# Images 0 and 1 in a new order on all engines of a binarized Winograd convolution

## The chip, the cores and the metric

The kernel runs on one core of a Trainium2 chip. The metric is the time of one execution on the device in microseconds. Three executions of the kernel before gave a median of 950.4 us (949.73 to 950.79).

## The reference

The input is 16 images of 256 channels of 56 x 56 in fp32. What is computed, cut to its core:

```
v    = group_norm(x)                         # 32 groups, per image
xn   = batch_norm(v) * gamma + beta          # statistics over all 16 images
t    = sign(xn)                              # 1 or -1, never 0
csum = sum over channels of clip(xn, -1, 1) * t
y    = conv3x3(t, w) + b                     # 256 to 256 channels, padding 1
bmap = (box3x3(csum) + beta_b) / (box3x3(256) + beta_b)
out  = x + y * bmap
```

Both normalizations fold into one factor and one offset for each channel and image (tile AB), which are known only after all of x has been read once.

## The kernel before, in words

**Before the images.** Until about 151 us the kernel reads x once for the statistics (VectorE), and prepares the weights as fp16 pairs for a one-dimensional Winograd scheme (tile U, GpSimd and ScalarE). A chain of small VectorE operations ends at L721 with AB, the semaphore coef_ready. Then the 16 images are worked off, each in four groups g = 0 to 3. On the input side a group is one half h = g // 2 of the rows and one channel half c = g % 2. On the output side it is one half of the rows and one half of the output channels.

**Input side of a group.** ScalarE makes u = sign(AB * x) (`sign`, L385). `planes` (L395, L397) makes T = relu(2u) and T8 = 4T - 3. For image 0 VectorE makes T and T8 itself (L736, L741). VectorE's `transform` then makes differences (T with L739, tile D with L744 and L746) and from them the six planes of tile V (L750 for planes 0 and 1, L752 for positions 2 and 4, L753 for positions 3 and 5). T, T8 and D are single tiles. `v_ready` counts finished groups.

**Products.** TensorE runs 72 matmuls for a group in three sets of 24: `first`, `second`, `third`, each for two of the six planes, both channel halves, three horizontal shifts and two digits of the weights, accumulating in PSUM tile acc, of which there are two halves (b = g % 2). The first set needs just the V positions that L752 writes. A first set may begin when VectorE has emptied the bank two groups back (`y03_done`). Between the sets ScalarE copies acc to sn (`snapshot`, L427): second waits for the snapshot of the first set (snap1), third for the snapshot of the second (snap2). The order on TensorE is first(g), third(g-1), second(g).

**Output side.** `mid` (L790, L795, L797) combines the snapshots into two of the four output rows, `ends` (L806 twice) reads acc after the third set and gives the other two rows and y03_done, `finish` (L818) adds the bias and multiplies by the map bmap. GpSimd's queue then adds x by an accumulating DMA (L325) and stores (L320), two transfers of 784 KB for each group. SyncE does the last group's store.

**Channel sums.** ScalarE makes abs(xn) (`absolute`, L406) and a complement (L412), VectorE `pair_sum` (L760) joins the channel halves in ssum, `fold` (L767) reduces ssum to 49 columns of quarter for each half of the rows. TensorE's `quarter_sums` (L526) multiplies quarter by a folding matrix, one fp32 matmul for each half. ScalarE's `channel_sums` (L419) brings the result to cs49, SyncE stores it and reads it back by rows into crow (`crow_load`), and VectorE's `beta_map` (L773 to L782) makes the map, which SyncE stores and broadcasts to bmap.

**Order.** Each engine's order is written out by hand. Image 0 and parts of image 1 are straight code, then a loop runs over pairs of images. Each engine's queue is in order, so a waiting instruction holds all behind it. SyncE's queue holds the loads of x for image n + 2, crow_load, map_store and map_load. Image 0's order on TensorE before:

```
first(0, 0, 0, by_channels=True)
first(0, 0, 1)
second(0, 0, 0)
third(0, 0, 0)
second(0, 0, 1)
quarter_sums(0, 0)
quarter_sums(0, 1)
pe.wait_ge(v_ready, 4)
first(0, 0, 2)
```

With by_channels the first 12 matmuls use only channel half 0 and wait for v_ready 1, the next 12 for v_ready 2.

Of the kernel before, what the change touches and what calls it, by code (L numbers as in the profile page):

```python
# [42 lines left out]
def conv_preact(nc, x, w_t, gamma, beta, conv_b, beta_b, consts, sum_rows, map_rows, out):  # L43
# [6 lines left out]
    with ExitStack() as ctx:  # L50
# [3 lines left out]
        def sem(name):  # L54
# [18 lines left out]
        cs49 = sb("cs49", [NB, 2, SQ])  # L73
# [17 lines left out]
        ab = sb("ab", [P, 2, 2, CT])  # L91

        spare = ssum[:, :]
# [28 lines left out]
        ab_ready, u_ready, t_ready, t4_ready, t8_ready, cq_done, aq_done, v_ready = (  # L122
            sem(s) for s in ("ab_ready", "u_ready", "t_ready", "t4_ready", "t8_ready", "cq_done", "aq_done",
                             "v_ready"))
        quarter_ready = sem("quarter_ready")
# [47 lines left out]

        block = ctx.enter_context(nc.Block())
# [3 lines left out]
        def _(sp):  # L178
# [24 lines left out]
            def crow_load(m):  # L203

                sp.wait_ge(cs8_ready, m + 1)
                sp.dma_start(sum_rows[m, W:W + H * W].rearrange("(h k f) -> k h f", h=2, f=SQ), cs49[:, :, :])\
                  .then_inc(cs_stored, 16)
                sp.wait_ge(cs_stored, 16 * m + 16)
                at_least(sp, vsum_ready, m)
                sp.dma_start(crow[:, :, 1:W + 1], row_windows[m].rearrange("r (k w) -> r k w", w=W))\  # L210
                  .then_inc(crow_in, 16)

            def load(n, src, g):

                if g == 3:
                    sp.wait_ge(u_ready, 4 * n + 8)
                if g < 3 or isinstance(n, int) and n == 0:
                    sp.wait_ge(abs_done, 4 * n + g + 5)
                load_rows(src, g)

            def first_load(g):

                sp.wait_ge(u_ready, g + 1)
                sp.wait_ge(abs_done, g + 1)
                load_rows(x_rows[1], g)
# [30 lines left out]
            for g in range(G4):  # L256
                first_load(g)
            sp.wait_ge(zeros_in, 16)
# [4 lines left out]
            for g in range(G4):  # L263
                load(0, x_rows[2], g)
# [67 lines left out]
        def _(act):  # L332
# [56 lines left out]
            def planes(m, g):  # L389
# [4 lines left out]
                act.wait_ge(u_ready, s + 1)  # L394
                nc.scalar.activation(T[:, 30:60], u[:, g % 2, h:h + HR + 2], ACT.Relu, scale=2.0).then_inc(t_ready, 1)  # L395
                act.wait_ge(t_ready, s + 1)
                nc.scalar.activation(T8[:, :], T[:, 30:30 + HR], ACT.Copy, scale=4.0, bias=-3.0).then_inc(t8_ready, 1)  # L397

            def absolute(m, a, g):
# [3 lines left out]
                if g < 3:  # L403
                    act.wait_ge(u_ready, 4 * m + g + 1)
# [10 lines left out]
            def channel_sums(m):  # L415

                act.wait_ge(cs_done, 2 * m + 2)
                at_least(act, cs_stored, 16 * m)
                nc.scalar.activation(cs49[:, :, :].rearrange("p h f -> p (h f)"), csum[0:NB, 0:2 * SQ],  # L419
                                     ACT.Copy, bias=float(P)).then_inc(cs8_ready, 1)  # L420

            def snapshot(n, g, half):
# [3 lines left out]
                at_least(act, mid_done, s - 1)  # L426
                nc.scalar.activation(sn[:, b, half], acc[:, b, :, 0:N], ACT.Copy, scale=inv_s[:, b:b + 1])\  # L427
# [6 lines left out]
            sign(0, 0, 0)  # L434
# [32 lines left out]
            def image(n, a):  # L467
                for g in range(G4):
                    snapshot(n - 1, 3, 1) if g == 0 else snapshot(n, g - 1, 1)
                    planes(n, 3) if g == 0 else planes(n + 1, g - 1)  # L470
                    if g == 0:
                        channel_sums(n)
                        coefficients(n + 1, 1 - a)
                    snapshot(n, g, 0)
                    sign(n + 1, 1 - a, g)
                    for k in ((0,), (1,), (2, 3), ())[g]:
# [4 lines left out]
            with act.Fori(0, (NI - 2) // 2) as i:  # L481
                image(2 * i + 1, 1)
                image(2 * i + 2, 0)
            for g in range(G4):
                snapshot(NI - 2, 3, 1) if g == 0 else snapshot(NI - 1, g - 1, 1)
                if g == 0:
                    planes(NI - 1, 3)
                    channel_sums(NI - 1)
                snapshot(NI - 1, g, 0)
# [4 lines left out]
        def _(pe):  # L494
# [34 lines left out]
            def products(n, a, g, planes, done, by_channels=False):  # L529

                h, co = g // 2, g % 2
                for part in range(CT if by_channels else 1):
                    if by_channels:
                        pe.wait_ge(v_ready, part + 1)
                    for bank, k in enumerate(planes):
# [10 lines left out]
                last.then_inc(done, 1)  # L546

            def first(n, a, g, by_channels=False):

                at_least(pe, y03_done, 4 * n + g - 1)  # L550
                products(n, a, g, FIRST, first_done, by_channels)
# [11 lines left out]
            def image(n, a):  # L563
                for g in range(G4):
# [3 lines left out]
                    if g == 0:  # L568
                        quarter_sums(n, 0)
                        quarter_sums(n, 1)  # L570
# [29 lines left out]
        def _(dve):  # L600
# [123 lines left out]
            def transform(m, a, g):  # L724

                c, h, s = g % 2, g // 2, 4 * m + g
                pair = lambda at: T[:, at:at + 62].rearrange("p (j r) w -> p j r w", j=2)[:, :, 0:28:4]
                rows = lambda t, at: t.rearrange("p (q i) w -> p i q w", i=4)[:, at:at + 2]
                both = lambda at: D[:, :, at:HR:4]
                vk = lambda first, step: V[:, a, c, first:first + step + 1:step, h].rearrange(  # L730
                    "p k (q w) -> p k q w", w=W)
                at_least(dve, v_ready, s)
                at_least(dve, cq_done, s)
                if isinstance(m, int) and m == 0:
                    dve.wait_ge(u_ready, s + 1)
# [4 lines left out]
                if isinstance(m, int) and m == 0:  # L740
# [3 lines left out]
                nc.vector.tensor_tensor(rows(D[:, 1], 1), pair(3), pair(1), ALU.subtract).then_inc(aq_done, 1)  # L744
                dve.wait_ge(t8_ready, s + 1)
                nc.vector.tensor_tensor(D[:, 0], T[:, 32:32 + HR], T8[:, :], ALU.subtract).then_inc(cq_done, 1)  # L746
                if not (isinstance(m, int) and m <= 1):
                    dve.wait_ge(third_done, 4 * m - 6 + 2 * h)
                dve.wait_ge(cq_done, s + 1)
                nc.vector.tensor_tensor(vk(0, 1), rows(D[:, 0], 2), rows(D[:, 0], 0), ALU.subtract)  # L750
                dve.wait_ge(aq_done, s + 1)
# [176 lines left out]
```

## Time and profile before

| | |
|---|---|
| median of three executions | 950.4 us |
| the profiled execution's own time | 950.02 us |
| its span, first to last instruction | 948.0 us |
| PE busy with matmuls | 787.4 us, 83% |
| DVE busy | 790.3 us, 83% |
| ACT busy | 587.7 us, 62% |
| mean granted TensorE clock | 0.929 |

The profile is of one execution. PE is TensorE, PEld its weight loads, DVE VectorE, ACT ScalarE, POOL GpSimd and SP SyncE. In a timeline, consecutive instructions of one group are merged to a row with a count, and the bracket tells the idle time of the engine before it and what ended it. Matmul times overlap: a row of n matmuls lasts n steps and one latency, so a step is read from the starts of two rows. The granted clock is 1.00 at 2.4 GHz and 0.50 at 1.2 GHz. The shares of the whole span say little here, since the statistics stage ends near 151 us and the products only begin then.

### The profile page before, as it was taken

The page shows a single profiled execution, that of the slowest core. Times are in us where ns is not written, and L with a number is a line of the kernel's source. Part 1 is how long each engine was busy: PE and PEld are TensorE (multiplying, and loading weights), DVE is VectorE, ACT ScalarE, POOL GpSimd, SP SyncE. Part 2 cuts the span into 40 slices and gives each one's busy share as a digit, 9 for nine tenths or more (in the row PEclk, how much of TensorE's full clock was granted, in tenths as well). Part 3 has the DMA queues.
Part 4 walks back from the last instruction along what each step waited for, and adds up shares of the span by engine and source line. Part 5 has one row for each costly group of instructions (what it writes and reads, how often), then busy time and mean ns, then how long its engine had stood idle before and what let it go on. Part 6 is the DMA issues. An engine that isn't in the chain of part 4 may idle for free. (4 is left out here: it accounts for less than half of the span.)

```text
span 948.0 us, 12800 instructions
## 1 busy us (share of the span) xinstructions
PE 787.4 (83%) x4718; PEld 464.2 (49%) x4718; DVE 790.3 (83%) x1240; ACT 587.7 (62%) x472; POOL 141.2 (15%) x160
## 2 busy tenths in 40 slices
PE   2100003999999999999999999999999999999996
PEld 2100002555555555555555555555555555555553
DVE  4999997979879797979797979797979797979764
ACT  2043105796777777777777868686868686868410
POOL 0089300001111111111111111111111110101021
PEclk9655556999999999999999999999999999999998
DMA  9999972258978797969696969696969696968587
GB/s 361 428 402 378 418 291 71 74 207 239 281 201 283 173 309 167 314 165 303 169 309 166 305 169 302 175 282 188 285 193 287 185 289 190 280 167 208 134 237 239
DMA packets 43362, 232.76 MB, mean 246 GB/s; under 512 B 10448, under 2 KB 10576, under 8 KB 39248
## 3 DMA queue, kind: packets, MB, share of 16 engines
q0 software_dynamic: 18144, 101.16, 41.2%
q1 hardware_dynamic: 24432, 131.25, 38.4%
q10 hardware_dynamic: 768, 0.12, 0.1%
q8 instruction: 9, 0.15, 0.1%
q14 instruction: 9, 0.07, 0.0%
HBM read 180.73 MB, written 51.79 MB: 245 GB/s over the span
## 5 line engine op out<-in xcount | busy, mean ns | idle before, releaser
L540 PE MATMUL acc<-V,U 128*128 128x385 f16 (+1 forms) x4608 | 771.0, 330 | 18.4 <-DVE V L753 12.6
L540 PEld LDWEIGHTS acc<-V,U 128*128 128x128 f16 x4608 | 449.5, 98 | 333.9 <-issue 13.3
L427 ACT ACTIVATE sn<-acc,inv_s 128x784 f32<-128x784 f32 x128 | 116.8, 913 | 203.4 <-PE acc L540 200.2
L325 POOL DMA_DIRECT2D y<-x x63 | 53.9, 856 | 720.0 <-DVE y L818 706.5
L818 DVE SCALAR_TENSOR_TENSOR y<-y,vec,bmap 128x1568 f32<-128x1568 f32 (+1 forms) x65 | 117.5, 1810 | 0.4
L406 ACT ACTIVATE r<-xb,ab 128x1568 f32<-128x1568 f32 x64 | 106.5, 1690 | 6.7 <-DVE ssum L760 3.1
L385 ACT ACTIVATE u<-xb,ab 128x1624 f16<-128x1624 f32 x64 | 110.5, 1730 | 0.1
L395 ACT ACTIVATE T<-u 128x1680 f16<-128x1680 f16 x60 | 95.6, 1594 | 5.1 <-DVE D L746 5.0
L397 ACT ACTIVATE T<-T 128x1568 f16<-128x1568 f16 x60 | 90.6, 1511 | 1.9
L512 PE MATMUL csum<-mv,cst 128*128 128x32 f32 x2 | 0.6, 396 | 94.9 <-DVE mv L622 94.9
L746 DVE TENSOR_TENSOR D<-T 128x1568 f16<-128x1568 f16 x64 | 62.3, 974 | 18.1 <-ACT T L397 18.0
L790 DVE SCALAR_TENSOR_TENSOR ds<-sn 128x784 f32<-128x784 f32 x64 | 62.0, 969 | 6.6 <-ACT sn L427 6.6
L630 DVE BATCH_NORM_STATS2 st<-y 128x6 f32<-128x448 f32 x112 | 60.2, 601 | 6.2 <-DMA y<-x 6.1
L760 DVE SCALAR_TENSOR_TENSOR ssum<-r 128x1568 f32<-128x1568 f32 x32 | 57.3, 1792 | 8.2 <-issue 5.2
L630 DVE BATCH_NORM_STATS2 st<-xb 128x6 f32<-128x448 f32 x98 | 52.6, 600 | 6.8 <-DMA xb<-x 6.8
L767 DVE TRANSPOSE_TENSOR_REDUCE quarter<-ssum 128x49 f32<-128x1568 f32 x32 | 57.7, 1805 | 0.1
L320 POOL DMA_DIRECT2D out<-y x63 | 52.1, 826 | 29.3 <-DMA y<-x 28.8
L739 DVE TENSOR_SCALAR T<-T 128x784 f16<-128x784 f16 x64 | 22.5, 351 | 35.3 <-ACT T L395 35.2
L412 ACT ACTIVATE r<-r 128x1568 f32<-128x1568 f32 x32 | 48.3, 1511 | 1.0
L806 DVE SCALAR_TENSOR_TENSOR y<-acc,inv_s,ds 128x392 f32<-128x392 f32 x64 | 39.7, 621 | 10.0 <-PE acc L540 9.9
L512 PEld LDWEIGHTS csum<-mv,cst 128*128 128x128 f32 x2 | 0.5, 313 | 94.9 <-issue 94.9
L795 DVE SCALAR_TENSOR_TENSOR y<-sn,ds 128x392 f32<-128x392 f32 x64 | 36.4, 568 | 10.0 <-DMA out<-y 3.4
(92 smaller groups left out, 392.8 us busy)
## 6 DMA issues: line engine op xcount, KB each, us to landing
xb<-x SPq DMA_DIRECT2D x64, 812.0 KB, 6.4
y<-x POOLq DMA_DIRECT2D x63, 784.0 KB, 9.2
out<-y POOLq DMA_DIRECT2D x63, 784.0 KB, 9.3
y<-x SPq DMA_DIRECT2D x16, 1568.0 KB, 8.1
bmap<-map_rows SPq DMA_DIRECT2D x32, 784.0 KB, 5.9
xb<-x SPq DMA_DIRECT2D x14, 1568.0 KB, 8.4
V<-w_t SPq DMA_DIRECT2D x2, 1152.0 KB, 14.5
out<-y SPq DMA_DIRECT2D x2, 392.0 KB, 2.4
```

Source lines behind the costliest of these rows:

```text
L385: nc.scalar.activation(u[:, g % 2, 1:1 + XR], by_row(xb[:, c, g // 2]), ACT.Sign, scale=ab[:, a, 0, c:c + 1], bias=ab[:, a, 1, c:c + 1])\
L395: nc.scalar.activation(T[:, 30:60], u[:, g % 2, h:h + HR + 2], ACT.Relu, scale=2.0).then_inc(t_ready, 1)
L397: nc.scalar.activation(T8[:, :], T[:, 30:30 + HR], ACT.Copy, scale=4.0, bias=-3.0).then_inc(t8_ready, 1)
L406: nc.scalar.activation(r[:, c, 0:HPX], own_rows(g), ACT.Abs, scale=ab[:, a, 0, c:c + 1], bias=ab[:, a, 1, c:c + 1]).then_inc(abs_done, 1)
L427: nc.scalar.activation(sn[:, b, half], acc[:, b, :, 0:N], ACT.Copy, scale=inv_s[:, b:b + 1])\
L540: last = nc.tensor.matmul(by_row(acc[:, g % 2, bank, 0:N])[:, :, lo:hi], U[:, ci, digits, k, dx, co * P:(co + 1) * P], by_row(V[:, a, ci, ...
L630: ins = nc.vector.bn_stats(st[:, a, c, j], stat_buffer(a, c)[:, j * PIECE:(j + 1) * PIECE])
L746: nc.vector.tensor_tensor(D[:, 0], T[:, 32:32 + HR], T8[:, :], ALU.subtract).then_inc(cq_done, 1)
L760: nc.vector.scalar_tensor_tensor(out=ssum[:, :], in0=r[:, 0, 0:HPX], scalar=1.0, in1=r[:, 1, 0:HPX], op0=ALU.min, op1=ALU.subtract).then_i ...
L767: nc.vector.tensor_reduce(quarter[:, h, :], ssum[:, :].rearrange("p (b i) -> p b i", i=SQ), AX.X, ALU.add, apply_transpose=True).then_inc( ...
L790: nc.vector.scalar_tensor_tensor(out=ds[:, :, :], in0=sn[:, b, 0], scalar=2.0, in1=sn[:, b, 1], op0=ALU.mult, op1=ALU.subtract).then_inc(d ...
L818: nc.vector.scalar_tensor_tensor(out=y[:, g, lo:hi], in0=y[:, g, lo:hi], scalar=vec[:, 2, b:b + 1], in1=bmap[:, h, lo:hi], op0=ALU.add, op ...
```

## The change

Five things are changed for images 0 and 1, two for all images.

1. VectorE makes the signs of image 0's group 0 itself (`sign_first`, one fp32 comparison giving 1 or 0, with a one-column negation before it). ScalarE begins with group 1. u_ready is counted without group 0.
2. VectorE makes the differences of group 0 into D00 (a view of sn), writes its first planes (the L752 operation), then those of group 1 (v_first), and only then the other planes of both.
3. TensorE's first set of group 1 is split: plane 1 before second(0, 0, 0), plane 3 behind it. quarter_sums(0) moves behind first(0, 0, 2).
4. VectorE's and ScalarE's orders of images 0 and 1 are rewritten. VectorE makes T8 also for groups 1 and 2 of image 1. Image 1 and image 14 are taken out of the loops of those two engines; TensorE's loop stays.
5. SyncE issues the loads of image 2's groups 0 and 1 ahead of crow_load(0).
6. In all images the two folding matmuls become one with 98 columns of quarter, whose result lies on 98 partitions in cs98. In ScalarE's loop channel_sums stands behind snapshot(n, 0, 0) and no longer ahead of it.
7. In image 15, VectorE's finish of groups (14, 3), (15, 0) and (15, 1) come one step later each.

```
 TensorE
-            def quarter_sums(m, h):
-                pe.wait_ge(quarter_ready, 2 * m + h + 1)
-                if h == 0:
-                    at_least(pe, cs8_ready, m)
-                nc.tensor.matmul(csum[0:NB, h * SQ:(h + 1) * SQ], quarter[:, h, :], cst[:, C_FOLD:C_FOLD + SQ],
-                                 start=True, stop=True).then_inc(cs_done, 1)
+            def quarter_sums(m):
+                pe.wait_ge(quarter_ready, 2 * m + 2)
+                at_least(pe, cs8_ready, m)
+                nc.tensor.matmul(csum[0:2 * NB, 0:SQ], quarter[:, :, :].rearrange("p h b -> p (h b)"),
+                                 cst[:, C_FOLD:C_FOLD + SQ], start=True, stop=True).then_inc(cs_done, 1)
...
             first(0, 0, 0, by_channels=True)
-            first(0, 0, 1)
+            first(0, 0, 1, banks=(0,))
+            pe.wait_ge(v_ready, 2)
             second(0, 0, 0)
+            first(0, 0, 1, banks=(1,))
             third(0, 0, 0)
             second(0, 0, 1)
-            quarter_sums(0, 0)
-            quarter_sums(0, 1)
             pe.wait_ge(v_ready, 4)
             first(0, 0, 2)
+            quarter_sums(0)
 VectorE
+            def sign_first():
+                dve.wait_ge(x_in[0], 16)
+                chain(nc.vector.tensor_scalar(neg_b[:, :], AB[:, 0, 1, 0:1], -1.0, None, ALU.mult))
+                nc.vector.tensor_scalar(u[:, 0, 1:1 + XR], by_row(xb[:, 0, 0]), AB[:, 0, 0, 0:1], neg_b[:, 0:1],
+                                        ALU.mult, ALU.is_gt).then_inc(u0_ready, 1)
...
-            transform(0, 0, 0)
-            transform(0, 0, 1)
-            transform(0, 0, 2)
+            sign_first()
+            differences(0, 0, D00)
+            first_planes(0, 0, 0, D00).then_inc(v_first, 1)
+            differences(0, 1, D)
+            first_planes(0, 0, 1, D).then_inc(v_first, 1)
+            other_planes(0, 0, 0, D00)
+            other_planes(0, 0, 1, D)
             pair_sum(0, 0)
             fold(0, 0)
+            transform(0, 0, 2)
+            mid(0, 0)
             transform(0, 0, 3)
+            ends(0, 0)
             pair_sum(0, 1)
-            mid(0, 0)
-            ends(0, 0)
             fold(0, 1)
             mid(0, 1)
             transform(1, 1, 0)
-            beta_map(0)
             ends(0, 1)
             pair_sum(1, 0)
+            beta_map(0)
             transform(1, 1, 1)
             mid(0, 2)
             fold(1, 0)
-            transform(1, 1, 2)
             ends(0, 2)
+            finish(0, 0)
             pair_sum(1, 1)
             fold(1, 1)
-            finish(0, 0)
+            transform(1, 1, 2)
+            finish(0, 1)
+            mid(0, 3)
+            ends(0, 3)
+            transform(1, 1, 3)
+            beta_map(1)
...
+            finish(last - 1, 2)
+            mid(last, 0)
+            ends(last, 0)
+            finish(last - 1, 3)
+            mid(last, 1)
+            ends(last, 1)
+            finish(last, 0)
+            mid(last, 2)
+            finish(last, 1)
+            ends(last, 2)
+            finish(last, 2)
 ScalarE
             coefficients(0, 0)
-            sign(0, 0, 0)
             sign(0, 0, 1)
...
+            complement(0, 1)
+            snapshot(0, 0, 1)
             snapshot(0, 1, 0)
-            snapshot(0, 0, 1)
-            complement(0, 1)
             coefficients(1, 1)
             sign(1, 1, 0)
+            sign(1, 1, 1)
             planes(1, 0)
-            sign(1, 1, 1)
             snapshot(0, 1, 1)
-            channel_sums(0)
-            planes(1, 1)
-            snapshot(0, 2, 0)
             absolute(1, 1, 0)
             absolute(1, 1, 1)
+            snapshot(0, 2, 0)
+            channel_sums(0)
             complement(1, 0)
+            planes(1, 1)
             sign(1, 1, 2)
             snapshot(0, 2, 1)
-            planes(1, 2)
+            absolute(1, 1, 2)
             snapshot(0, 3, 0)
-            sign(1, 1, 3)
-            absolute(1, 1, 2)
             absolute(1, 1, 3)
             complement(1, 1)
+            planes(1, 2)
+            sign(1, 1, 3)
 SyncE
             for g in range(G4):
                 first_load(g)
+            load(0, x_rows[2], 0)
+            load(0, x_rows[2], 1)
             sp.wait_ge(zeros_in, 16)
             crow_load(0)
             map_store(0)
             map_load(0, 0)
             map_load(0, 1)
-            for g in range(G4):
-                load(0, x_rows[2], g)
+            load(0, x_rows[2], 2)
+            load(0, x_rows[2], 3)
```

## Rows read from the trace of the kernel before

**Rows 1.** waits of PE between 210 and 940 us (total us, times, longest us).

```profile
PE acc L540 <- DVE y L806: 1.6, 1, 1.6
```

**Rows 2.** timeline of PE, 150 to 235 us (start us, us, engine, line, operation, tiles, count, idle before).

```profile
158.32 3.51 PE L540 MATMUL acc<-V,U 128*128 128x392 f16 x12 [11.78 <-DVE V L753]
162.65 10.14 PE L540 MATMUL acc<-V,U 128*128 128x392 f16 x60 [0.83 <-DVE V L753]
173.80 8.15 PE L540 MATMUL acc<-V,U 128*128 128x392 f16 x48 [1.01 <-ACT sn L427]
...
190.79 12.13 PE L540 MATMUL acc<-V,U 128*128 128x392 f16 x72 [0.46 <-ACT sn L427]
...
208.75 4.16 PE L540 MATMUL acc<-V,U 128*128 128x392 f16 x24 [1.46 <-DVE y L806]
...
213.41 8.15 PE L540 MATMUL acc<-V,U 128*128 128x392 f16 x48
223.20 11.97 PE L540 MATMUL acc<-V,U 128*128 128x392 f16 x71 [1.64 <-DVE y L806]
```

**Rows 3.** timeline of PE inside the loop, 255 to 365 us.

```profile
311.42 0.37 PE L526 MATMUL csum<-cst,quarter 128*49 128x32 f32 x4
311.72 48.01 PE L540 MATMUL acc<-V,U 128*128 128x392 f16 x288
359.66 0.37 PE L526 MATMUL csum<-cst,quarter 128*49 128x32 f32 x4
```

**Rows 4.** timeline of DVE, 150 to 235 us, first transform.

```profile
151.43 0.22 DVE L721 TENSOR_TENSOR AB<-ssum,AB 128x32 f32<-128x32 f32 x1
153.78 0.60 DVE L736 TENSOR_SCALAR T<-u 128x1680 f16<-128x1680 f16 x1 [2.14 <-ACT u L385]
...
155.65 0.97 DVE L746 TENSOR_TENSOR D<-T 128x1568 f16<-128x1568 f16 x1
...
157.61 0.56 DVE L753 TENSOR_TENSOR V<-D 128x784 f16<-128x784 f16 x1
158.21 0.60 DVE L736 TENSOR_SCALAR T<-u 128x1680 f16<-128x1680 f16 x1
```

**Rows 5.** line L654, a one-source fp32 operation (duration ns min/median/max, start, shape).

```profile
L654 DVE TENSOR_SCALAR bmap<-bmap x1: 293/293/293, 48.1 to 48.1; 128x256 f32<-128x256 f32 x1
```

**Rows 6.** window 158 to 162 us (busy us by engine, granted clock, DMA share, GB/s).

```profile
158.00:162.00 4.00, 3.51 (x12) 1.51 (x12) 3.90 (x8) 3.97 (x4) 0.00 (x0) 0.61 0.60 188
```

**Rows 7.** timeline of DVE, 216 to 226 us, one group's work in the loop.

```profile
216.56 0.36 DVE L739 TENSOR_SCALAR T<-T 128x784 f16<-128x784 f16 x1
...
219.95 0.97 DVE L790 SCALAR_TENSOR_TENSOR ds<-sn 128x784 f32<-128x784 f32 x1
...
221.99 0.62 DVE L806 SCALAR_TENSOR_TENSOR y<-acc,inv_s,ds 128x392 f32<-128x392 f32 x1
...
223.06 0.33 DVE L773 TENSOR_REDUCE vsum<-crow 56x58 f32<-56x174 f32 x1
...
224.11 1.84 DVE L818 SCALAR_TENSOR_TENSOR y<-y,vec,bmap 128x1568 f32<-128x1568 f32 x1
```

**Rows 8.** page, costliest groups (busy us, mean ns of one, idle before).

```profile
L427 ACT ACTIVATE sn<-acc,inv_s 128x784 f32<-128x784 f32 x128 | 116.8, 913 | 203.4 <-PE acc L540 200.2
...
L760 DVE SCALAR_TENSOR_TENSOR ssum<-r 128x1568 f32<-128x1568 f32 x32 | 57.3, 1792 | 8.2 <-issue 5.2
...
L767 DVE TRANSPOSE_TENSOR_REDUCE quarter<-ssum 128x49 f32<-128x1568 f32 x32 | 57.7, 1805 | 0.1
```

**Rows 9.** waits of DVE between 240 and 900 us.

```profile
DVE vsum L773 <- DMA crow<-sum_rows: 33.5, 13, 2.9
```

**Rows 10.** timeline of DVE, 300 to 365 us, last write of group 0.

```profile
329.00 0.62 DVE L806 SCALAR_TENSOR_TENSOR y<-acc,inv,ds 128x392 f32<-128x392 f32 x1
```

**Rows 11.** timeline of POOL, 870 to 950 us, the last store it issues.

```profile
941.14 0.55 POOL L320 DMA_DIRECT2D out<-y  x1 [5.59 <-DMA y<-x]
```

**Rows 12.** window 939 to 942 us, columns as in the other window.

```profile
939.00:942.00 3.00, 0.85 (x6) 0.29 (x3) 2.02 (x3) 0.00 (x0) 0.55 (x1) 1.00 0.99 328
```

More of the change, by code:

```diff
@@ L479, in image @@
                             complement(n + 1, k // 2)
[L481 to L489, printed above, removed]
+            last = NI - 1
+            begin(1, 1, late_planes=True)
+            proceed(1, 1)
+            with act.Fori(0, (NI - 4) // 2) as i:
+                begin(2 * i + 2, 0)
+                proceed(2 * i + 2, 0)
+                begin(2 * i + 3, 1)
+                proceed(2 * i + 3, 1)
+            begin(last - 1, 0)
+            proceed(last - 1, 0)
+            snapshot(last - 1, 3, 1)
+            planes(last, 3)
+            snapshot(last, 0, 0)
+            channel_sums(last)
+            for g in range(1, G4):
+                snapshot(last, g - 1, 1)
+                snapshot(last, g, 0)
             snapshot(NI - 1, 3, 1)
@@ L533, in products @@
                     if by_channels:
-                        pe.wait_ge(v_ready, part + 1)
-                    for bank, k in enumerate(planes):
+                        pe.wait_ge(v_first, part + 1)
+                    for bank in banks:
+                        k = planes[bank]
                         for i, (ci, digits, dx) in enumerate(TERMS):
@@ L847, in _ @@
             fold(1, 0)
-            transform(1, 1, 2)
             ends(0, 2)
+            finish(0, 0)
             pair_sum(1, 1)
             fold(1, 1)
-            finish(0, 0)
-            def image(n, a, prep=True):
-                before = lambda g, back: (n, g - back) if g >= back else (n - 1, 4 + g - back)
-                for g in range(G4):
-                    if prep:
-                        finish(*before(g, 3))
-                    else:
-                        for late in ((3,), (3, 2), (2,), (2,))[g]:
-                            finish(*before(g, late))
-                    if prep and g == 3:
+            transform(1, 1, 2)
@@ L863, in image, with proceed @@
+            finish(0, 1)
[3 more added lines that the diff above has]
+            beta_map(1)
+            def proceed(n, a):
+                before = lambda g, back: (n, g - back) if g >= back else (n - 1, 4 + g - back)
+                for g in range(1, G4):
+                    finish(*before(g, 3))
+                    if g == 3:
                         pair_sum(n + 1, 1)
-                    if prep and g == 2:
+                    if g == 2:
                         fold(n + 1, 0)
-                    if g == 0:
-                        transform(n, a, 3)
-                    elif prep:
-                        transform(n + 1, 1 - a, g - 1)
@@ L870, in image @@
-                    mid(*before(g, 1))
-                    ends(*before(g, 1))
-                    if g == 0:
-                        beta_map(n)
-                    if prep and g == 1:
+                    transform(n + 1, 1 - a, g - 1)
+                    mid(n, g - 1)
+                    ends(n, g - 1)
+                    if g == 1:
                         pair_sum(n + 1, 0)
-                    if prep and g == 3:
+                    if g == 3:
                         fold(n + 1, 1)
-            with dve.Fori(0, (NI - 2) // 2) as i:
-                image(2 * i + 1, 1)
-                image(2 * i + 2, 0)
@@ L882, in _, with begin @@
-            image(NI - 1, 1, prep=False)
-            finish(NI - 1, 2)
+            def begin(n, a):
+                finish(n - 1, 1)
+                transform(n, a, 3)
+                mid(n - 1, 3)
+                ends(n - 1, 3)
+                beta_map(n)
+            last = NI - 1
+            proceed(1, 1)
+            with dve.Fori(0, (NI - 4) // 2) as i:
+                begin(2 * i + 2, 0)
+                proceed(2 * i + 2, 0)
+                begin(2 * i + 3, 1)
+                proceed(2 * i + 3, 1)
```

133 lines of the change are left out of this document (83 added, 50 removed).

## The prediction

> **What bounds the kernel now.** I read the waits of PE first. From 210 us to 940 us it waits once, 1.6 us near 223 us [rows 1]. Inside the loop 288 matmuls take 47.94 us, 166.5 ns each, then comes the fold, 0.30 us from its start to the next product, and nothing else [rows 3]. So a gain in the loop can come only from less work on PE, and a gain elsewhere only from an earlier start of the products or from gaps before 223.2 us.
>
> The timeline of PE shows these [rows 2]. Products start at 158.32 us. From there to 223.20 us the program has 336 matmuls (264 for image 0 without its last third set, 72 after it). At 166.5 ns they need 55.9 us, two folds 0.6. The window 158 to 162 us has a mean clock of 0.61 [rows 6], so PE ran at 1.2 GHz until about 161.1 us, 2.8 us after its start, and half of these 2.8 us, 1.4, is lost. The elapsed time is 64.9 us, so 64.9 - 55.9 - 0.6 - 1.4 = 7.0 us are gaps. The rows show them: 1.0 before 162.65 (group 1's V late), 1.15 before 173.80 (snapshot late, ScalarE stood behind the pair sum), some 0.7 before 190.79, 2.0 over the stretch from 190.79 to 208.75, 1.8 before 223.20 (VectorE's y late), the rest small.
>
> In front of the first product stands a chain on two engines [rows 4]: AB ready at 151.65, sign on ScalarE, T begun on VectorE at 153.78, V complete at 158.17, PE 0.15 later.
>
> **Start of the products.** AB is ready at 151.65. The negation is one small chained operation, 0.25 us (the step of a chained operation of this size is that to the end of L721). The sign on VectorE has 1,624 fp32 elements. No row shows it. L654, one source and fp32, takes 0.293 us for 256 elements [rows 5]; the two-source L760 takes 1.79 us for 1,568 [rows 8]. From these two alone the price per element would be 1.14 ns, and L654's fixed part zero. If instead both have a fixed part of 0.16, as the 0.22 us of L721 with its 32 columns suggests [rows 4], L760 costs 1.04 ns per element and L654 0.52, which gives 0.16 + 1,624 x 0.52 = 1.0 us for the sign. The bounds are 1.0 and 1.85 (the rate of L760). I take 1.0, as L654 is the nearer form. T then begins at 152.95. From T to the end of L746 are 2.85 us [rows 4], the first planes of group 0 start at 155.8 and take 0.56 like L753, v_first is 1 at 156.4, PE starts at 156.5. **Start 1.8 us earlier**: 0.85 from the sign, 0.95 from the two plane operations that no longer stand ahead. With a sign of 1.85 us it is 1.0.
>
> **Group 1.** Its differences and first planes follow, 3.4 us, ready at 159.7. PE's 12 matmuls of channel half 0 last until 159.9 if the clock again rises 2.8 us after the start (159.3); the first gap is gone. Plane 1 of group 1 runs 161.9 to 163.9, which covers the snapshot of group 0 (0.91, ready at 163.1) and the other planes, 4 x 0.48 us, ready 161.6. Then second(0) to 167.9, plane 3 to 169.9, during which the second snapshot is taken at 168.3. The second gap is gone too. If the clock rose no sooner than before, at 161.1, the loss is half of 4.6 instead of 1.4, so 0.9 worse; I take 1.4 and keep 0.9 for the range.
>
> **The rest of image 0, image 1.** VectorE decides. Prices, as steps from start to start: a transform without conversions 3.4, with T8 3.9, with both 4.4; mid 2.0, ends 1.07, beta_map 1.05, finish 1.8 [rows 4, 7]; pair_sum and fold 1.8 each [rows 8]. In the new order, from 161.6 on:
> pair_sum, fold, transform(0,2), mid(0,0), transform(0,3), ends(0,0) end at 177.2; first(0,2) wants it at 177.9. Slack 0.7.
> pair_sum, fold (180.7, wanted 181.9), mid(0,1), transform(1,0) to 186.1; ends(0,1) waits for third(0,1), 186.35, ends 187.4, wanted 190.15.
> pair_sum 189.2, beta_map 190.3, transform(1,1) with T8 194.2, mid(0,2), fold 198.0, ends(0,2) 199.4, wanted 202.15.
> finish, pair_sum, fold 204.8, wanted by the fold on PE at 206.15. transform(1,2) with T8, finish, mid, ends(0,3) 213.6, wanted 214.4.
> transform(1,3), beta_map, finish, transform(2,0), mid(1,0), ends(1,0) 226.4, wanted at 226.3. Slack 0.
> Each is in time, so **all 7.0 us of gaps go**, the last one by nothing. PE reaches first(1,2) at 156.5 + 408 x 0.1665 + 1.4 + 0.5 = 226.3, against 223.20 + 72 x 0.1665 = 235.2 before. Two places have no slack or nearly none, and waits add their own latencies of 0.1 to 0.2, so I put 0.5 us back.
>
> **The late edge of this** is beta_map(0). Loads of 812 KB for image 2 now stand ahead of the sums in SyncE's queue. DVE's wait in the loop, 2.6 us each [rows 9], shows that such a small store and load can come late behind big ones. Here VectorE gets to it at 189.2 with 6 us after channel_sums. Up to 2.5 us late it would push ends(1,0) by as much and give PE up to 1.5 to 2 us of new gap; zero if the store lands quickly. ScalarE's own steps end over a microsecond ahead of what needs them, as a snapshot takes 0.91 [rows 8] within a set of 4.0 us. The extra T8 on VectorE (2 x 0.48) is in the sums above.
>
> **Fold.** Four passes (two fp32 matmuls, each two instructions) with 49 columns cost 0.30 us of PE [rows 3]. Two passes with 98 columns cost between 0.15 (a fixed price per pass) and 0.30 (by columns). I take the middle, 0.22: 16 x 0.08 = **1.3 us**, bounds 0 and 2.4. The rows can't separate the two. The Trainium skill, "TensorE: Matmul & The Clock Gate", section "LDWEIGHTS (loading the stationary operand)", says that a load takes columns / 1.2 ns, so 4 x 41 and 2 x 82 ns, the same: by it nothing is gained here, and the sum would be 1.3 us higher. No row here shows a load of 98 columns.
>
> **Loop.** channel_sums behind the snapshot comes some 0.5 us later, so the crow wait of 2.6 us grows to about 3.1. In the loop group 0's y is complete at 329.62 [rows 10] and first(2) would want it at 311.72 + 120 x 0.1665 = 331.70 [rows 3]. Slack 2.1, so the cost is nothing; without that cover it would be 0.5 us for each of 14 images. The images taken out of the loops execute the same instructions, cost nothing.
>
> **Tail.** The end follows the last product: ends, finish, add, store, unchanged. But finish (15,0) and (15,1) come later, by a step, and the adds on POOL's queue with them, so one pair of transfers more falls in the last 25 us. The last add before had landed by 941.14 [rows 11] with the DMA engines 0.99 busy at 328 GB/s [rows 12]; 784 KB is 2.4 us of that. Cost between 0 (the end may hang on SyncE's small stores alone) and 2.4. I take 0.5.
>
> **Sum**, against the profiled execution's 950.02: - 1.8 - 7.0 + 0.5 - 1.3 + 0.5 = 940.9. Its span would be 938.9. The profiled run lies 0.4 below the median; that is within the spread, and I give **941.0**.
>
> **Rivals.**
> A. VectorE becomes the bound between 190 and 230 us: sign at 1.85, clock loss, sums late. It keeps the start and some gaps: 941.0 + 0.85 + 0.9 + 1.5 = 944.3. For it: the slack of 0 at 226 us. Against it: once in the loop, PE never waits for this engine [rows 1]. 0.20.
> B. The fold gains nothing (the rule above): 942.3. 0.25.
> C. The tail pays a whole transfer, 2.4: 942.9. For it: the rate there. 0.08.
> D. The gaps don't vanish but move, each wait replaced by one behind it, as VectorE's work up to 226 us is the same but for 1.5 us more: only the start and a few us remain, 946. Against it: the checkpoints above. 0.04.
> E. Slower: the sums' chain in the loop. If the store, now 0.5 us later, met POOL's two transfers so that crow came over 2.1 us later than now, the first set of group 2 would wait in each image. At 2.8 us later it costs 0.7 x 14 = 10 us and eats the gain; beyond, it is slower. Against it: the largest wait before was 2.9. 0.03.
> The forecast itself, 939.5 to 942, 0.40.
>
> **Range.** Low: all gains, fold at 0.15 (1.1 more), no new waits, no tail, 950.4 - 1.8 - 7.0 - 2.4 = 939.2, and a bit under. High: A's 944.3. With 938.9 to 944.4 about 0.1 each side at most stays out. A measurement of this kernel tells 0.2%, 1.9 us, from no change: faster 0.95, same 0.02, slower 0.03.
>
> **What would show it.** PE's first product at 156.5 in the trace after, no idle over 0.3 us between its two halves nor before second(0,1), the next wait, if any, near first(1,2). The sign on VectorE at 1.0. The fold at 0.22 from its start to the next product, and a loop period of 48.16 instead of 48.24. No wait of PE in the loop. A wrong prediction would show as waits of PE for DVE y between 190 and 240 us, or a loop with waits, or an idle stretch behind the last product longer than before.

## The result, and the profile after

The kernel after takes 937.72 us, the median of four executions (937.66 to 938.68), against 950.07 us in the same comparison. The ratio is 0.9873 with a 95% interval of 0.9861 to 0.9885: **1.3% faster, 12.35 us**. I had forecast 941.0 us with a range from 938.9 to 944.4. The direction was right; the time lies 1.2 us below the range. The profiled execution took 937.77 us, its span is 936.0 us against 948.0.

The timeline of PE after, from 150 us on (start us, us, engine, line, operation, tiles, count, idle before), answers to [rows 2]:

```profile
156.35 25.46 PE L570 MATMUL acc<-V,U 128*128 128x392 f16 x144 [10.13 <-DVE V L790]
181.65 0.28 PE L555 MATMUL csum<-cst,quarter 128*98 128x32 f32 x2
181.76 24.09 PE L570 MATMUL acc<-V,U 128*128 128x392 f16 x144
206.06 0.36 PE L555 MATMUL csum<-cst,quarter 128*98 128x32 f32 x2 [0.22 <-DVE quarter L826]
206.26 20.38 PE L570 MATMUL acc<-V,U 128*128 128x392 f16 x120
227.20 28.07 PE L570 MATMUL acc<-V,U 128*128 128x392 f16 x168 [0.56 <-DVE y L865]
```

What stood in seven pieces is now one block of 144 products, the fold (L555), and a second block of 144. Of the gaps of before, these rows show 0.22 us ahead of the second fold and 0.56 ahead of 227.20; what is left in all is counted further down. The loop, answering to [rows 3]:

```profile
255.10 0.28 PE L555 MATMUL csum<-cst,quarter 128*98 128x32 f32 x2
255.22 48.01 PE L570 MATMUL acc<-V,U 128*128 128x392 f16 x288
303.06 0.28 PE L555 MATMUL csum<-cst,quarter 128*98 128x32 f32 x2
303.18 48.01 PE L570 MATMUL acc<-V,U 128*128 128x392 f16 x288
```

The period from fold to fold is 303.06 - 255.10 = 47.96 us, against 48.24 before. The fold is followed by the next product after 0.12 us instead of 0.30, and the 288 products between take 303.06 - 255.22 = 47.84 instead of 47.94.

The spans divide as follows. The marks in PE's timelines are the fold of image 2, at 263.17 us before and 255.10 after, and the block of the last 24 products, at 935.69 and 923.67.

| stretch | before, us | after, us | difference |
|---|---|---|---|
| span's start to AB ready | 151.65 | 151.33 | -0.3 |
| AB to the first product | 6.67 | 5.02 | -1.65 |
| first product to the fold of image 2 | 104.85 | 98.75 | -6.1 |
| that fold to the last 24 products | 672.52 | 668.57 | -3.95 |
| last 24 products to the end | 12.31 | 12.33 | 0.0 |
| span | 948.0 | 936.0 | -12.0 |

The fourth row is the loop, 14 periods of 0.28 us each. I had put 14 x 0.08 = 1.1 there. The third row holds the two folds of images 0 and 1, about 0.5 us of its 6.1; the rest is gaps. The waits of PE after (total us, times, longest us):

```profile
PE acc L570 <- DVE V L790: 10.1, 1, 10.1
PE acc L570 <- ACT sn L442: 1.0, 1, 1.0
PE acc L570 <- DVE y L865: 0.6, 1, 0.6
PE csum L555 <- DVE quarter L826: 0.2, 1, 0.2
```

The first is the start of the products, the second stands ahead of the last 24 products and was there before, with the same 1.01 us.

### The profile page after: what moved, and what is told of

Read it like the earlier page. It is cut to its first block and busy times, and to the rows that moved or that the text cites. A ratio compares the mean times of both kernels' runs of the same rounds, so it can differ in the third digit from the quotient of the medians.

```text
span 936.0 us, 12745 instructions
## 1 busy us (share of the span) xinstructions
PE 782.9 (84%) x4686; PEld 464.9 (50%) x4686; DVE 790.4 (84%) x1244; ACT 581.3 (62%) x469; POOL 140.8 (15%) x160
## 5 line engine op out<-in xcount | busy, mean ns | idle before, releaser
L408 ACT ACTIVATE T<-T 128x1568 f16<-128x1568 f16 x58 | 87.6, 1510 | 1.8
```

## The experiments

Times of single executions scatter: of five executions of the unchanged kernel after, four took 937.4 to 938.5 us and one 942.5. So the medians below are read together with the profile of each, which shows where a difference lies. Where the intervals of two kernels overlap, their medians alone decide nothing.

### The fold: its passes, its waits, its columns

**Two folds in the kernel after.**

```
             def quarter_sums(m):
-                pe.wait_ge(quarter_ready, 2 * m + 2)
-                at_least(pe, cs8_ready, m)
-                nc.tensor.matmul(csum[0:2 * NB, 0:SQ], quarter[:, :, :].rearrange("p h b -> p (h b)"),
-                                 cst[:, C_FOLD:C_FOLD + SQ], start=True, stop=True).then_inc(cs_done, 1)
+                for h in range(2):
+                    pe.wait_ge(quarter_ready, 2 * m + h + 1)
+                    if h == 0:
+                        at_least(pe, cs8_ready, m)
+                    nc.tensor.matmul(csum[0:NB, h * SQ:(h + 1) * SQ], quarter[:, h, :], cst[:, C_FOLD:C_FOLD + SQ],
+                                     start=True, stop=True).then_inc(cs_done, 1)
```

With it ScalarE's copy and SyncE's store go back to the tile cs49 of before.

> The kernel after, with the two folding matmuls of before (49 columns each, a wait ahead of each, results in cs49) at the new place. My theory: the fold is the mis-sized term. From the traces the loop's period fell from 48.24 to 47.96 us, 0.28 an image, where I had put 0.08. If the fold alone did that, this kernel's loop has 48.24 again and its time is 937.7 + 16 x 0.28 = 942.2 us. Rival: the 0.28 comes from another edit (channel_sums behind the snapshot, the images taken out of the loops) and the fold is worth the 0.08 that I gave it: 939.0, period 48.04.

Measured: 943.55 us (942.72 to 944.29), ratio to before 0.9933 (0.9919 to 0.9946). The loop, in the timeline of PE:

```profile
229.20 28.07 PE L573 MATMUL acc<-V,U 128*128 128x392 f16 x168 [1.63 <-DVE y L868]
...
305.44 0.37 PE L558 MATMUL csum<-cst,quarter 128*49 128x32 f32 x4
...
353.69 0.37 PE L558 MATMUL csum<-cst,quarter 128*49 128x32 f32 x4
```

The period is 353.69 - 305.44 = 48.25 us, as before. So the loop's gain is the fold's alone, and the later place of channel_sums costs it nothing. The time is 1.3 us over what I expected. In the profile three things stand against that: PE starts 0.3 us later, waits 1.63 us ahead of 229.20 instead of 0.56, and the clock rose later, at 161.1 us, 4.4 us after the first product (156.69) instead of 2.85. At half the clock for 1.55 us more, PE loses 0.8. The window 161 to 162 us has a mean clock of 0.96 (the third number from the end), the one ahead of it 0.50:

```profile
161.00:162.00 1.00, 1.00 (x8) 0.55 (x7) 1.00 (x3) 0.89 (x1) 0.00 (x0) 0.96 0.82 221
```

The longer wait ahead of 229.20 goes with the sums. Between 178 and 240 us VectorE waits once for crow, 2.2 us here and 2.4 in the kernel after. There it is beta_map(0) that waits, ahead of 191.18, and here it is beta_map(1), ahead of 219.67:

```profile
DVE vsum L835 <- DMA crow<-sum_rows: 2.2, 1, 2.2
```

**Two folds with one wait.** As above, with both waits ahead of the first matmul and one signal behind the second.

```
+                pe.wait_ge(quarter_ready, 2 * m + 2)
+                at_least(pe, cs8_ready, m)
+                for h in range(2):
+                    last = nc.tensor.matmul(csum[0:NB, h * SQ:(h + 1) * SQ], quarter[:, h, :],
+                                            cst[:, C_FOLD:C_FOLD + SQ], start=True, stop=True)
+                last.then_inc(cs_done, 1)
```

> The kernel after, with two folding matmuls of 49 columns but all waits ahead of the first and one signal behind the second. Tells whether the second wait or the number of passes costs. In the trace after, the fold's first weight load starts 0.16 us ahead of its product and under the last product of the set; before, it started with it and 0.33 us of the weight loader's idle time lay in front. Theory one (the wait between the two matmuls holds the loads back): period about 48.0, time near 938.5. Theory two (four passes of 49 columns cost twice two of 98, whatever the waits): period 48.2, time near 942.

Measured: 945.59 us (944.25 to 946.35), ratio 0.9958 (0.9943 to 0.9973); the profiled execution, the fastest, has a span of 942.4.

```profile
305.54 0.37 PE L557 MATMUL csum<-cst,quarter 128*49 128x32 f32 x4
...
353.78 0.37 PE L557 MATMUL csum<-cst,quarter 128*49 128x32 f32 x4
```

The period is 48.24 again. The wait between the two costs nothing; theory one is out. The median lies 3.6 us above the 942 expected and 2 us above the kernel with two waits, though the two profiles agree within 0.4 us; what the slower executions spent isn't in a profile.

**One fold in the kernel before.** The same edit the other way round, with everything else as before.

> The kernel before with the one folding matmul of 98 columns alone, all orders as before. If the fold is worth 0.28 an image in the loop: 950.1 - 4.2 = 945.9 us and a period of 47.96. If only 0.08: 948.8. If the gain in the loop needed the new order, no change.

Measured: 945.82 us (945.53 to 946.07), ratio 0.9958 (0.9944 to 0.9971).

```profile
262.77 0.28 PE L523 MATMUL csum<-cst,quarter 128*98 128x32 f32 x2
...
310.72 0.28 PE L523 MATMUL csum<-cst,quarter 128*98 128x32 f32 x2
```

Period 47.95, 4.1 us saved in all. The fold needs no help from the new order, and the rest of the change is worth 945.8 - 937.7 = 8.1 us, or 943.6 - 936.0 = 7.6 by the spans of the two profiles.

**One fold of 49 columns.** This kernel leaves out the sums of the second half of the rows.

```
-                nc.tensor.matmul(csum[0:2 * NB, 0:SQ], quarter[:, :, :].rearrange("p h b -> p (h b)"),
+                nc.tensor.matmul(csum[0:NB, 0:SQ], quarter[:, 0, :],
                                  cst[:, C_FOLD:C_FOLD + SQ], start=True, stop=True).then_inc(cs_done, 1)
```

> The kernel after with one folding matmul of 49 columns, so that the sums of the second half of the rows are left out (a constant stands in their place). Tells what a column of the fold costs. If a pass has a fixed price and columns cost nothing: period 47.96 as in the kernel after, 937.7 us. If loads go by columns (98 against 49, two passes, 41 ns less each): up to 0.08 less, period 47.88, 936.4 us.

Measured: 942.36 us (941.09 to 944.38), ratio 0.9928 (0.9913 to 0.9943). Neither expectation held: with half the columns the kernel is slower.

```profile
303.82 0.28 PE L555 MATMUL csum<-cst,quarter 128*49 128x32 f32 x2
...
351.97 0.28 PE L555 MATMUL csum<-cst,quarter 128*49 128x32 f32 x2
```

The period is 48.15, 0.19 more than with 98 columns and 0.09 less than with two folds of 49 columns (48.24). So of the 0.28 us that the change gains in each image, halving the passes at 49 columns is worth 0.09 and the greater width the other 0.19. The timelines of the weight loader show where the two widths differ. With 49 columns, then with 98 in the kernel after:

```profile
303.82 0.17 PEld L555 LDWEIGHTS csum<-cst,quarter 128*49 128x49 f32 x2 [0.33 <-issue]
304.02 0.94 PEld L570 LDWEIGHTS acc<-V,U 128*128 128x128 f16 x7
```

```profile
302.90 0.33 PEld L555 LDWEIGHTS csum<-cst,quarter 128*98 128x98 f32 x2
303.09 0.85 PEld L570 LDWEIGHTS acc<-V,U 128*128 128x128 f16 x6
```

With 49 columns the load starts together with the fold's matmul at 303.82, after 0.33 us in which the loader did nothing. With 98 it starts at 302.90, 0.16 us ahead of the matmul at 303.06 and beneath the product in front. So a part of the load is no longer in the open.

**64 and 66 columns.** The edit is the same with `[:, 0:64]` and `[:, 0:66]` of quarter.

> The kernel after with one folding matmul of 64 columns; the sums of the other 34 columns are left out. What was seen: the period of the loop is 47.96 with 98 columns, 48.15 with 49 and 48.24 with two of 49, with one wait or two; with 98 the weight load begins under the last product, with 49 the loader is idle 0.33 us first. Theory: what counts is whether the fold has more than 64 columns. Then 64 behaves as 49: idle 0.33 us before the load, period 48.15 or a little more. Rival: the cost falls steadily with more columns: period near 48.1, between the two. The loop's period is what is read here.

> The same with 66 columns, the other 32 left out. Theory (more than 64): as 98, the load begins under the last product, period 47.96 or a few hundredths less. Rival (steadily): near 48.1, the same as 64.

One execution each, 941.8 and 938.5 us. The timelines of PE, 64 columns first:

```profile
256.14 0.30 PE L555 MATMUL csum<-cst,quarter 128*64 128x32 f32 x2
256.37 48.01 PE L570 MATMUL acc<-V,U 128*128 128x392 f16 x288
304.31 0.30 PE L555 MATMUL csum<-cst,quarter 128*64 128x32 f32 x2
```

```profile
256.10 0.25 PE L555 MATMUL csum<-cst,quarter 128*66 128x32 f32 x2
256.19 48.00 PE L570 MATMUL acc<-V,U 128*128 128x392 f16 x288
304.03 0.25 PE L555 MATMUL csum<-cst,quarter 128*66 128x32 f32 x2
```

Periods 48.17 and 47.93 us. Two columns more save 0.24 us, and they do so all along: from the fold of image 2 to the last 24 products are 671.6 and 668.2 us. The loader was idle 0.33 us ahead of the load with 64 columns and not with 66. A steady price per column is out: 15 columns more, from 49 to 64, change the period by 0.02, the next two by 0.24, the 32 from there to 98 by 0.03. There is a step between 64 and 66 columns.

**The fold of 98 columns twice.** Two identical matmuls behind the same waits.

> The kernel after with the folding matmul of 98 columns run twice, the second over the first's result. Prices two passes of 98 columns by themselves. If two passes of 98 cost what the first two do from start to next product (0.12 us): period 48.08. If most of that 0.12 is a one-off: 48.0. If loads of 98 columns cost 82 ns each: 48.12.

One execution, 941.01 us.

```profile
304.03 0.45 PE L556 MATMUL csum<-cst,quarter 128*98 128x32 f32 x4
304.32 48.00 PE L572 MATMUL acc<-V,U 128*128 128x392 f16 x288
352.16 0.45 PE L556 MATMUL csum<-cst,quarter 128*98 128x32 f32 x4
```

Period 48.13. Two more passes of 98 columns cost 0.17 us, nearest to the third case expected (48.12). Four passes of 98 columns, 0.29 us from start to product, take no longer than four of 49, 0.30.

### The start of the products

**The first sign on ScalarE.**

```
             coefficients(0, 0)
+            act.wait_ge(x_in[0], 16)
+            nc.scalar.activation(u[:, 0, 1:1 + XR], by_row(xb[:, 0, 0]), ACT.Sign, scale=ab[:, 0, 0, 0:1],
+                                 bias=ab[:, 0, 1, 0:1]).then_inc(u0_ready, 1)
             sign(0, 0, 1)
...
-            sign_first()
             differences(0, 0, D00)
```

> The kernel after with image 0's first sign back on ScalarE (1.73 us and a wait between engines) instead of the negation and comparison on VectorE (1.12). T would begin at 153.5 instead of 152.8 us, PE at 157.0 to 157.1 instead of 156.35. My theory: 0.65 to 0.7 us slower, 938.4, all engines shifted alike. Rival: ScalarE now begins group 1's sign 1.6 us later, which delays group 1 and its absolutes; T of group 1 wants u at 156.8 and gets it at 155, so no more than that. If the first products are not on the path: 937.7.

Measured: 939.32 us (938.66 to 942.64), ratio 0.9898 (0.9883 to 0.9914). PE starts at 157.28 instead of 156.35, and the span of 936.8 is 0.8 over the kernel after, with the clock's rise as early as there (2.8 us). The interval is wider than what is looked for, so the medians don't decide it. The profile's shift, 0.93 us at the first product and 0.8 in the span, is a little over the 0.65 to 0.7 expected, and it reaches the end: the first products are on the path.

**All planes of a group at once.**

```
-            first_planes(0, 0, 0, D00).then_inc(v_first, 1)
-            differences(0, 1, D)
-            first_planes(0, 0, 1, D).then_inc(v_first, 1)
+            first_planes(0, 0, 0, D00)
             other_planes(0, 0, 0, D00)
+            differences(0, 1, D)
+            first_planes(0, 0, 1, D)
             other_planes(0, 0, 1, D)
```

The first set of group 0 then waits on v_ready in place of v_first.

> The kernel after, but the planes of group 0 are all made before group 1's differences, and those of group 1 all before its channel half is used, as in the kernel before. PE still starts 0.95 us later than after (157.3) if it waits for all six planes, and has its 12 products of channel half 0 done at about 160.7, while group 1 is ready at 161.65: a gap of 0.9 us. By my theory 1.8 to 1.9 us slower, 939.6 (0.2 less if the clock rises in the gap). Rival: later stages give it back, since image 1 is bound by VectorE near 227 us, where PE waited 0.56 us; then the loss is 0.6 less, 939.0.

Measured: 939.76 us (939.23 to 944.08), ratio 0.9902 (0.9888 to 0.9916), beside 938.26 of the kernel after in the same rounds. The medians lie 1.5 us apart, between the two expectations, but the intervals overlap. The two profiled executions, whose clocks rose 4.3 and 4.2 us after the start, have spans of 937.7 and 936.7.

```profile
157.12 26.35 PE L570 MATMUL acc<-V,U 128*128 128x392 f16 x144 [11.08 <-DVE V L795]
183.30 0.28 PE L555 MATMUL csum<-cst,quarter 128*98 128x32 f32 x2
...
228.91 28.07 PE L570 MATMUL acc<-V,U 128*128 128x392 f16 x168 [0.56 <-DVE y L865]
```

PE starts 0.8 us later than in the kernel after. The gap of 0.9 between the channel halves, which my theory counted on, isn't there: it was worked out for a clock that rises 2.8 us after the start, and here it rose after 4.3, so the first 12 products took longer and covered most of the time until group 1 was ready. What the gap would be with an earlier rise isn't shown.

**The first set of group 1 in one piece.**

```
-            first(0, 0, 1, banks=(0,))
+            first(0, 0, 1)
             pe.wait_ge(v_ready, 2)
             second(0, 0, 0)
-            first(0, 0, 1, banks=(1,))
```

> The kernel after with group 1's first set in one piece ahead of second(0,0,0). The first snapshot is then well covered, but second(0,0,0) ends 2 us later and the snapshot behind it (0.2 + 0.91) lies in the open: a gap of 1.1 us before third(0,0,0), at 170 us. Theory: 1.1 us slower less the 0.56 and 0.2 that PE waits later anyway, so 938.1 to 938.8. Rival: VectorE sets the time at 227 us fully, and the gap costs only its excess over the 0.8 us of waits: 938.0.

Measured: 938.95 us (938.39 to 940.05), ratio 0.9886 (0.9872 to 0.99), beside 938.26.

```profile
170.84 12.13 PE L570 MATMUL acc<-V,U 128*128 128x392 f16 x72 [1.01 <-ACT sn L442]
...
206.96 20.30 PE L570 MATMUL acc<-V,U 128*128 128x392 f16 x120
227.83 28.07 PE L570 MATMUL acc<-V,U 128*128 128x392 f16 x168 [0.57 <-DVE y L864]
```

The gap came where it was expected, 1.01 us ahead of 170.84. In both profiled executions the clock rose 2.9 us after the start, so they can be laid side by side: the last row stands at 227.83 against 227.20. 0.6 of the 1.01 us is left; the wait of 0.22 ahead of the fold vanished. The medians can't tell 0.7 us.

### The sums of image 0, and the kernel after again

```
-            load(0, x_rows[2], 0)
-            load(0, x_rows[2], 1)
             sp.wait_ge(zeros_in, 16)
             crow_load(0)
...
-            load(0, x_rows[2], 2)
-            load(0, x_rows[2], 3)
+            for g in range(G4):
+                load(0, x_rows[2], g)
```

> The kernel after with all four loads of image 2 behind crow_load(0), map_store and map_load, as before. In the trace after, the store of the sums took 6.6 us to land behind two loads of 812 KB, beta_map(0) waited 2.4 us for it, and PE waited 0.22 us for the fold and 0.56 us for y. Theory: those two waits vanish: 0.8 us faster, 936.9. Rival: the loads, 12 us later, make ScalarE late with image 2's first sign (it stands at 211.2 us, loads would land near 200): not faster, or slower by what it waits.

> The kernel after once more, for a comparison on the same chip in the same rounds as the three beside it. Every theory: 937.7 us, with 0.85 us more in an execution in which PE's clock rises 4.4 instead of 2.85 us after its start.

Measured: 939.27 us (938.11 to 941.84), ratio 0.9887 (0.9875 to 0.99), with the loads late, and 938.26 us (937.41 to 942.54), ratio 0.9884 (0.9867 to 0.99), for the kernel after. No gain is shown. VectorE's waits for crow between 178 and 240 us, in the kernel after and then with the loads late:

```profile
DVE vsum L832 <- DMA crow<-sum_rows: 2.4, 1, 2.4
```

```profile
DVE vsum L830 <- DMA crow<-sum_rows: 1.8, 1, 1.8
```

```profile
189.96 0.34 DVE L830 TENSOR_REDUCE vsum<-crow 56x58 f32<-56x174 f32 x1
...
219.12 0.35 DVE L830 TENSOR_REDUCE vsum<-crow 56x58 f32<-56x174 f32 x1 [1.76 <-DMA crow<-sum_rows]
```

beta_map(0) at 189.96 waits no more, but beta_map(1) at 219.12 waits 1.76 us, and PE then waits 1.52 us for y ahead of its product at 228.65, against 0.56. The wait moved from one image to the next. Why beta_map(1)'s sums come late isn't shown. One reading is that its store shares the DMA engines with the loads of image 2, but the kernel with two folds has the same picture, 2.15 us at beta_map(1) and 1.63 on PE, with these loads where the kernel after has them. There beta_map(0) doesn't wait either: between SyncE's store of the sums from cs49 and its next load lie 4.0 us (184.03 to 188.04), against 6.6 in the kernel after, which stores the same sums from the 98 partitions of cs98 (182.92 to 189.53), and 2.85 with the loads late (184.16 to 187.01). So both the loads ahead of it and the new form of the store may hold the sums of image 0 back. The clock rose 5.6 us after the start in this execution, which cost 1.4 us more than in the kernel after and hides the rest.

## Why the prediction was wrong

**The failed step** is the fold: "I take the middle, 0.22: 16 x 0.08 = 1.3 us, bounds 0 and 2.4". It gives 0.28 us an image, 4.1 us in all by the kernel before with this edit alone. With 4.1 in place of 1.3 the forecast would have been 938.2. What failed is the reading that the gain lies between a price per pass and a price per column. Halving the passes is worth 0.09, close to the 0.08 put, but the greater width, which could only be nothing or a loss in that sum, gained another 0.19. The upper bound of 2.4 failed too: it took the fold's whole cost as the 0.30 us from its start to the next product [rows 3], divided by passes. Two things lay outside. The 288 products in front shrank from 47.94 to 47.84, so 0.10 us of the fold's cost stood ahead of its start, where I had read it as products. And the load of 98 columns starts beneath the last product, so of the two passes just 0.12 us is in the open. I divided what the rows showed, and the change altered what they don't show.

The rule of the Trainium skill that I weighed ("TensorE: Matmul & The Clock Gate", section "LDWEIGHTS (loading the stationary operand)") gives columns / 1.2 ns. Single loads agree in their slope: 124 ns with 49 columns and 167 with 98, 0.88 ns a column, beside a fixed part of some 80 ns that the rule doesn't have. What I drew from it, no gain, didn't come. The table ahead of the first section of that page of the Trainium skill says that the queue pulls loads ahead of matmuls in flight. For the fold's own load the trace agrees with 66 and 98 columns, and with 49 and 64 it doesn't; between 49 and 98 columns the period fell by 0.19 us although the loads are longer.

```profile
L526 PEld LDWEIGHTS csum<-cst,quarter x64: 120/124/126, 181.9 to 890.5; 128*49 128x49 f32 x64
```

```profile
L555 PEld LDWEIGHTS csum<-cst,quarter x32: 162/167/167, 181.5 to 878.5; 128*98 128x98 f32 x32
```

**Start of the products**: 1.8 earlier forecast, 1.65 measured from AB. The sign (L811) took 1.12 us for 1.0, 0.69 ns for each of its 1,624 elements against the 1.14 of L760; the upper bound of 1.85 is out.

```profile
151.61 1.12 DVE L811 TENSOR_SCALAR u<-xb,AB,neg_b 128x1624 f16<-128x1624 f32 x1
...
155.64 0.57 DVE L790 TENSOR_TENSOR V<-sn 128x784 f16<-128x784 f16 x1
...
158.99 0.57 DVE L790 TENSOR_TENSOR V<-D 128x784 f16<-128x784 f16 x1
```

The two first planes (L790) stand at 155.64 and 158.99, as worked out (155.8 and 159.1).

**The gaps**: 7.0 us to go, 0.5 back. After, the rows show 0.22 and 0.56 us of idle time, 0.8 in all. Counted as in the prediction, more is left. From 156.35 to 227.20 are 70.85 us; 408 products at 47.84 / 288 = 0.1661 us take 67.8, two folds 0.24, the clock 1.4, and 1.4 remains. So 5.6 us of gaps went and not the 6.5 of the sum, and this error of 0.9 hid a part of the fold's: the forecast came nearer than its fold term deserved. The waits stand where the checkpoints had least slack: the one ahead of 227.20 is the checkpoint at 226.3 with slack 0. beta_map(0) waited 2.37 us for crow, as its late edge said ("Up to 2.5 us late").

```profile
191.18 0.35 DVE L832 TENSOR_REDUCE vsum<-crow 56x58 f32<-56x174 f32 x1 [2.37 <-DMA crow<-sum_rows]
```

From there to 227 us VectorE waits for nothing more, and its y comes at 227.06, so this wait stands in the chain that ends with PE's 0.56 us. No run shows PE without it: where beta_map(0) didn't wait, beta_map(1) did. The cost stayed under the 1.5 to 2 us that I had bounded it with. The experiments test the sign, the order of the first planes, the split of the first set (by its gap of 1.01 us), the order of the loads and the fold. The new orders of VectorE and ScalarE behind that and of image 15 were not run alone, so which of them closed which of the later gaps isn't shown.

**The clock** rose 2.85 us after the first product in the profiled execution, near the 2.8 of before (the stretch 160 to 161 us stands at 1.00). In the profiles of the experiments it took 2.8 to 5.6 us. The 0.9 us that I kept for this belongs in the range, and 1.4 would have been nearer. What decides when the clock rises isn't shown.

```profile
156.00:160.00 4.00, 3.65 (x14) 1.82 (x15) 3.93 (x9) 3.97 (x4) 0.00 (x0) 0.60 0.53 159
160.00:161.00 1.00, 1.00 (x8) 0.59 (x6) 1.00 (x4) 1.00 (x1) 0.00 (x0) 1.00 0.97 286
```

**The tail**: 0.5 us put, nothing measured. 12.31 us from the last 24 products to the end before, 12.33 after. The later adds of group (15, 0) and (15, 1) were not on the path.

```profile
929.70 0.55 POOL L330 DMA_DIRECT2D out<-y  x1 [5.71 <-DMA y<-x]
```

POOL's last store waited 5.71 us for its add, against 5.59 [rows 11], and goes out 6.3 us ahead of the end instead of 6.9.

**The loop's sums**: channel_sums behind the snapshot cost PE nothing. DVE's waits for crow went from 33.5 us in 13 [rows 9] to 37.3 in 14, so 2.7 each where 3.1 was expected, and PE waits for nothing in the loop:

```profile
DVE vsum L832 <- DMA crow<-sum_rows: 37.3, 14, 3.8
```

Of the rivals, A (VectorE the bound, 944.3) came in its mechanism, from 191 to 227 us, but at a price of 0.56 us on PE; C, D and E didn't come. B, no gain by the fold, was wrong in the other direction. A rival in which the wider fold gains more than its halved passes was missing. As a check, the misses add up: the span fell by 12.0 us where the sum has 9.1, and the difference of 2.9 is 3.2 from the fold (16 x 0.28 = 4.5 by the periods, for 1.3), 0.5 from the tail, 0.3 from AB, less 0.15 from the start and 0.9 from the gaps. Shown are the worth of the fold, the step between 64 and 66 columns and that the load starts early above it. Why the loader treats the two sides differently isn't shown: columns of weights and rows written in PSUM go together in all these kernels.

## What to carry to other kernels

When a small matmul stands in a stream of large ones, price it as the difference of two periods of the stream, not as the time from its start to the next product, and look in the weight loader's row for an idle stretch ahead of its load. Two narrow fp32 matmuls put side by side in one were worth 0.28 us each time here, 0.09 by the halved passes and 0.19 by the width, with which the load starts early; the wide one cost less than one of half its columns. When a start is tightened, list the slack at each checkpoint: the wait that remained ahead of 227.20 lay at the point with none, and when the sums of image 0 came in time, the wait stood at the next image instead. And add up all terms after the result, also when the total is near: here a gap term 0.9 us too high stood against a fold term 3.2 us too low.

## What was not expected of the hardware

- A fold of 64 columns gives a period of 48.17 us, one of 66 columns 47.93, one of 49 48.15, one of 98 47.96. With 49 and 64 columns the weight loader was idle 0.33 us in front of the load; with 66 and 98 the load began beneath the product in front.
- From the first product to the rise of the clock it took 2.8 us in some executions and up to 5.6 in others of almost the same program, which is worth up to 1.4 us.
- Executions of one kernel on the same chip went from 937.4 to 942.5 us with no edit between them.
